# Four adds a batch between neighbouring u buffers: from GpSimd instructions to accumulating DMAs

## The chip, the cores and the metric

One core of one Trainium2 chip runs the whole program. The metric is the device time of one execution, in microseconds (us). The profile gives a span (first to last instruction) of one profiled execution and that execution's own time beside it.

## What is computed

One decoder layer over x of 16 batches x 224 tokens x 512 features, in fp32, with a layer norm after each of three sublayers:

- a selective state-space block: in-projection to 1024 channels (xi) and 1024 gates (z), a causal convolution of four taps, silu, then per channel d and state n (16 states) the scan `h[t] = exp(delta[t] * A[d, n]) * h[t-1] + delta[t] * B[t, n] * xc[t, d]` and the output `y[t, d] = sum over n of h[t] * C[t, n]`, plus `xc * Dp`, times silu(z), then the out-projection;
- a context sublayer: a projection of the rows plus a decayed running sum over the context rows;
- a mixture of 8 experts with top-1 routing: each token's row is scattered to its expert's slots, two matrix products with a relu between them, the results scattered back.

The change lies in `y[t, d] = sum over n`. The sum over the 16 states is taken as 4 groups of 4 states, and each group's products `h * C` are summed by TensorE into a PSUM bank with an identity matrix as weights.

## The kernel before

The program works through the batches in steps. In one step, the scan of batch b, the projections of batch b+1, the output side of batch b-1 and the routing of batch b-2 run beside each other; `run_steps` unrolls the steps, and each engine's `body(b, par)` weaves its share of the scan (`main`, once for each of 32 slots) with side jobs. The order on each engine is fixed by hand: tables `PE_AT`, `ACT_AT`, `DVE_AT` and `POOL_AT` give each side job the slot after which it is issued (`woven`, `together`). Once the batches are done, the experts follow (from about 1,920 us on), and the change touches nothing there.

A slot s is one of KB = 8 channel blocks (k = s // 4) times Q = 4 groups of four states (q = s % 4). All its tiles are 128 partitions x 896 fp32 (four states x 224 tokens), 448 KB, 3,584 bytes in each partition. For every slot:

- POOL (GpSimd) writes `u = dx * B` into one of UB = 6 buffers (L968). The buffer is that of slot s - 6; the wait ahead of it is `sum_done >= b*32 + s - 5`, so the sums through slot s - 6 must be done (the count moves by one for each slot).
- ACT writes the four decays into the PSUM ring (L817).
- DVE runs the scan (L1260) and then the product with C back into the u buffer (L1269). For the seven slots in `POOLED` (1, 5, 9, 13, 17, 21, 25) DVE leaves the states in the u buffer, and POOL makes the product two slots later, after it has made u(s+2) (L973).
- PE sums the slot into its y bank with matmuls of the identity (L1585, eight records for each slot); the last of them moves `sum_done`.

For the four slots in `ADDED` (5, 9, 13, 17) POOL adds the neighbour's product: right behind its own product of slot a it adds u(a-1) onto u(a) (L979), once its own product is written (`multiplied`) and DVE's product of slot a-1 is there (`product_made(pool, b, s - 3)`). PE then leaves slot a-1 out (L1581 returns from `main`), sums slot a alone and moves `sum_done` by 2. So u(a+5), which goes into the buffer of slot a-1, waits for PE's sum of slot a.

`product_made(eng, b, s)` is the wait for a slot's product: `pooled_ready` for the seven slots, `p_ready` for the others. PE calls it for every slot that it sums; ACT only for slots outside POOLED (for those inside it waits for the scan); SP for slots 28 to 31. POOL's queue also issues two indirect DMAs a batch, the scatter of the routed rows (L930), and in the experts the scatter of results (L992). SP's queue issues all loads: among them `in_x` (448 KB) once a batch around slot 12 and eight of `bc_rows` (448 KB each) around the end of a batch. Around the scan POOL also makes delta in four pieces (L897, L899, L901, L904; three of them at slots 4, 4 and 12, in `late_steps`), the context rows (L942) and the normalised rows (L952).

Of the kernel before, what the change touches and what calls it, by code (L numbers as in the profile page):

```python
# [14 lines left out]
def build_decoder(nc, t):  # L15
# [5 lines left out]
    ALU, ACT, AX = mybir.AluOpType, mybir.ActivationFunctionType, mybir.AxisListType.X  # L21
# [25 lines left out]
    u_of = lambda b, s: (b * SLOTS + s) % UB  # L47
# [10 lines left out]
    with ctx:  # L58
# [79 lines left out]
        def flat(name):  # L138
            o, n = plan[name]
            return arena[:, o:o + n]  # L140

        bc = flat("bc").rearrange("p (w n l) -> p w n l", w=2, n=NS)
        u = flat("u").rearrange("p (k n l) -> p k n l", k=UB, n=QN)
        u_flat = flat("u").rearrange("p (k m) -> p k m", k=UB)
# [33 lines left out]
        for g in range(NG):  # L178
# [54 lines left out]
        bc_loaded = [sem(f"bc_loaded{q}") for q in range(Q)]  # L233
        sp_step, sp_ready, dl_step, delta_done = map(sem, (
            "softplus_step", "softplus_ready", "delta_step", "delta_done"))
        decay_ready, u_ready, scan_done, p_ready, pooled_ready, sum_done, y_done, skip_ready, multiplied, y_plain = map(sem, (
            "decay_ready", "u_ready", "scan_done", "p_ready", "pooled_ready", "sum_done", "y_done", "skip_ready", "pooled_multiplied",
            "y_written_whole"))
        x_res_loaded, ctx_loaded, ctx_step, ctx_ready = map(sem, ("x_res_loaded", "ctx_loaded", "ctx_step", "ctx_ready"))
        g_exp = sem("depool_exp")  # L240
# [13 lines left out]
        def need(eng, s, value):  # L254

            if not isinstance(value, int) or value > 0:
                eng.wait_ge(s, value)

        def apart(eng):


            eng.sem_inc(wait_kept, 1)
# [71 lines left out]
        def job_copied(eng, step, name):  # L334

            k, before_it = job(step, name)
            eng.wait_ge(w_free[k], before_it + 1)
# [13 lines left out]
        def stages(step):  # L351

            if isinstance(step, int):
                return 0 <= step + 2 < NB, 0 <= step + 1 < NB, 0 <= step < NB, 0 <= step - 1 < NB, 0 <= step - 2 < NB
            return True, True, True, True, True

        POOLED = tuple(range(1, SLOTS - Q, 4))
        MADE = SLOTS - len(POOLED)
        ADDED = (5, 9, 13, 17)
        made = lambda s: s + 1 - sum(p <= s for p in POOLED)  # L360
        pooled = lambda s: sum(p <= s for p in POOLED)

        def product_made(eng, b, s):

            if s in POOLED:
                eng.wait_ge(pooled_ready, b * len(POOLED) + pooled(s))
            else:
                need(eng, p_ready, b * MADE + made(s))

# [520 lines left out]
        @block.gpsimd  # L890
        def _(pool):
            def make_delta(tt, j, par):

                n, k = tt * 12 + 3 * j, slice(2 * j, 2 * j + 2)
                relu, corr = (delta[:, k], dx[:, k]) if j < PAIRS - 1 else (sp3[:, 0], sp3[:, 1])
                pool.wait_ge(sp_ready, tt * 2 + (j // 2 + 1))
                nc.gpsimd.tensor_tensor(w1p[:, k], w1p[:, k], corr, ALU.subtract).then_inc(dl_step, 1)  # L897
                pool.wait_ge(dl_step, n + 1)
                nc.gpsimd.tensor_tensor(delta[:, k], relu, w1p[:, k], ALU.add).then_inc(dl_step, 1)  # L899
                pool.wait_ge(dl_step, n + 2)  # L900
                nc.gpsimd.tensor_tensor(dx[:, k], delta[:, k], xc[:, par, k], ALU.mult).then_inc(dl_step, 1)  # L901
                pool.wait_ge(dl_step, n + 3)
                apart(pool)
                nc.gpsimd.memset(delta[:, k, 0:1], BIG_STEP).then_inc(delta_done, 1)  # L904

            def side(b, par):
                pre, pro, scan, epi, tail = stages(b)
                nxt, e, e2 = b + 1, b - 1, b - 2

                def late_steps():  # L910

                    for j in (1, 2, 3):
                        yield f"delta{j}"
                        make_delta(b, j, par)

                def first_steps():

                    yield "delta0"
                    make_delta(nxt, 0, 1 - par)

                def scatter():

                    yield "scatter"
                    pool.wait_ge(rt_step, e2 * 13 + 13)
                    job_copied(pool, b, "rank")
                    pool.wait_ge(normed, e2 * 2 + 2)
                    pool.wait_ge(token_set, e2 + 1)
                    apart(pool)
                    for h in range(2):
                        nc.gpsimd.indirect_dma_start(  # L930
                            out=xe_dram, out_offset=bass.IndirectOffsetOnAxis(ap=slot_i[:, h:h + 1], axis=0),
                            in_=x2e[:, h, :], in_offset=None, bounds_check=E * CAP - 1, oob_is_err=False,
                        ).then_inc(scattered, 16)

                def context():

                    yield "ctx"
                    pool.wait_ge(ctx_step, e * 11 + 8)
                    if isinstance(b, int) and b == 1:
                        pool.wait_ge(s_wrest, 16 * 6)  # L940
                    v = ctxt[0:H, :, 0:D]
                    nc.gpsimd.tensor_tensor(v, v, g_bc[:].unsqueeze(1).to_broadcast([H, 2, D]), ALU.mult).then_inc(ctx_ready, 1)  # L942

                def next_rows():

                    yield "xn"
                    pool.wait_ge(rinv_ready, b + 3)
                    if pro:
                        k, n = job(b, "z3")
                        pool.wait_ge(w_full[k], n + 1)  # L950
                        apart(pool)
                    nc.gpsimd.tensor_tensor(xn, xT, rinv[:, 1:2, :].to_broadcast([P, DC, L]), ALU.mult).then_inc(xn_ready, 1)  # L952

                return together(POOL_DRAIN if not scan and not pre else POOL_AT, *(part() for part, there in (
                    (late_steps, scan), (first_steps, pro), (scatter, tail), (context, epi), (next_rows, pre)) if there))

            def body(b, par):
                def main(s):

                    k, q = s // Q, s % Q  # L960
                    need(pool, sum_done, b * SLOTS + s - UB + 1)
                    if isinstance(b, int) and b == 0 and s == 0:
                        pool.wait_ge(s_rows, 16)
                    if s < Q:
                        pool.wait_ge(bc_loaded[q], b * 32 + 32)
                    if s % (2 * Q) == 0:
                        pool.wait_ge(delta_done, b * 4 + (s // (2 * Q) + 1))
                    nc.gpsimd.tensor_tensor(u[:, u_of(b, s)], dx[:, k:k + 1, :].to_broadcast([P, QN, L]),  # L968
                                            bc[:, 0, q * QN:(q + 1) * QN, :], ALU.mult).then_inc(u_ready, 1)
                    if s - 2 in POOLED:  # L970
                        q = (s - 2) % Q
                        pool.wait_ge(scan_done, b * SLOTS + (s - 1))
                        nc.gpsimd.tensor_tensor(u[:, u_of(b, s - 2)], u[:, u_of(b, s - 2)], bc[:, 1, q * QN:(q + 1) * QN, :], ALU.mult  # L973
                                                ).then_inc(pooled_ready if s - 2 not in ADDED else multiplied, 1)
                    if s - 2 in ADDED:
                        pool.wait_ge(multiplied, b * len(ADDED) + (ADDED.index(s - 2) + 1))
                        apart(pool)
                        product_made(pool, b, s - 3)
                        nc.gpsimd.tensor_tensor(u[:, u_of(b, s - 2)], u[:, u_of(b, s - 2)], u[:, u_of(b, s - 3)], ALU.add  # L979
                                                ).then_inc(pooled_ready, 1)  # L980

                woven(side(b, par), main, stages(b)[2])

            run_steps(pool, body)

            pool.wait_ge(out0_stored, NB * 32)
            def expert(e, par):
                pool.wait_ge(ids_ready, e + 1)
                for m in range(CM):
                    pool.wait_ge(mm_step, e * (3 * CM) + (3 * m + 3))  # L990
                    apart(pool)
                    nc.gpsimd.indirect_dma_start(  # L992
                        out=out_rows, out_offset=bass.IndirectOffsetOnAxis(ap=ids[:, par, m:m + 1], axis=0),
                        in_=res[m], in_offset=None, bounds_check=NB * L - 1, oob_is_err=False,
                    ).then_inc(out_scattered[m % 2], 16)

            with pool.Fori(0, E - 1, 2) as i:
                expert(i, 0)
                expert(i + 1, 1)
# [742 lines left out]
```

## Time and profile before

| | us |
|---|---|
| runs | 2616.44, 2612.46, 2616.50 (median 2616.44) |
| the profiled execution | 2609.2 |
| its span | 2607.4 |
| busy over the span: PE / DVE / POOL / ACT | 2414.4 / 2080.3 / 1786.6 / 1751.3 |
| mean granted TensorE clock | 0.963 |

Busy shares over the whole span mix two stages: the batches (to about 1,900 us), in which PE, DVE and POOL all work, and the experts behind them, in which PE alone is full. They are to be read stage by stage. A wait row reads: engine and line that waited, after the arrow the one that ended the wait, then the total us, how often, and the longest.

### The profile page before, as it was taken

What the parts mean: (1) busy time and instruction counts of PE and PEld (TensorE: products, weight loads), DVE (VectorE), ACT (ScalarE), POOL (GpSimd) and SP (SyncE); (2) the same over time, 40 slices, a digit from 0 to 9 for tenths busy, and PEclk for the clock granted to TensorE, in tenths of its full rate; (3) what the DMA queues carried; (4) which work ended last, traced back from release to release, by engine and by line L of the source; (5) the groups of instructions that cost most, each with busy time, mean ns of one, the idle gap of its engine ahead of it and who ended that gap; (6) DMA issues with size and microseconds to landing.
All of it is one profiled execution on the core that took longest, in us unless ns stands there. A gap on an engine that the chain in (4) does not pass through costs nothing.

```text
span 2607.4 us, 33255 instructions
## 1 busy us (share of the span) xinstructions
PE 2414.4 (93%) x11291; PEld 2048.7 (79%) x11291; DVE 2080.3 (80%) x2288; ACT 1751.3 (67%) x4011; POOL 1786.6 (69%) x1044
## 2 busy tenths in 40 slices
PE   6788999999999999999999999997869999999997
PEld 6686887878778787877878787775659999999996
DVE  4998999999999999999999999998633455444452
ACT  5667888888888888888888888886533333333331
POOL 1989999999999999999999999999410101000100
PEclk9898999999999999999999999997979999999998
DMA  6041202203021220202113020220233333234320
GB/s 212 8 144 56 85 16 85 81 27 93 15 85 43 65 89 12 92 16 85 59 49 89 12 93 18 75 82 19 96 108 124 130 126 126 97 129 138 136 75 18
DMA packets 90852, 202.62 MB, mean 78 GB/s; under 512 B 7948, under 2 KB 16794, under 8 KB 90702
## 3 DMA queue, kind: packets, MB, share of 16 engines
q1 hardware_dynamic: 81486, 179.21, 21.3%
q0 software_dynamic: 5120, 14.21, 1.7%
q10 hardware_dynamic: 4096, 7.34, 0.9%
q8 instruction: 77, 1.26, 0.2%
q14 instruction: 73, 0.60, 0.1%
HBM read 171.32 MB, written 29.95 MB: 77 GB/s over the span
## 4 chain that ended last, share of the span: by engine, by line
POOL 40%; PE 37%; DVE 8%; issue 6%; ACT 5%; DMA 3%; SPq 0%; POOLq 0%; DVEq 0%; ACTq 0%
POOL arena L968 23%; PE work L1604 12%; PE ring L1604 11%; POOL arena L973 6%; PE y L1585 4%; POOL arena L979 4%; DVE ring L1260 4%; PE work L1393 3%; DMA arena<-bc_rows 3%; POOL arena L901 2%; POOL arena L899 2%; POOL arena L897 2%; PE work L1416 2%; ACT ring L817 2%; DVE arena L1269 2%
## 5 line engine op out<-in xcount | busy, mean ns | idle before, releaser
L968 POOL TENSOR_TENSOR arena<-arena 128x896 f32<-128x896 f32 x512 | 1056.6, 2090 | 15.8 <-DMA arena<-bc_rows 10.5
L817 ACT ACTIVATE ring<-arena,small 128x224 f32<-128x224 f32 x2048 | 794.9, 436 | 146.0 <-DVE arena L1269 114.9
L1585 PE MATMUL y<-arena,cst_sb 128*128 128x224 f32 x3584 | 772.2, 367 | 91.7 <-POOL arena L979 64.9
L1260 DVE TENSOR_TENSOR_SCAN ring<-ring,arena 128x896 f32<-128x896 f32 x400 | 809.3, 2023 | 50.3 <-POOL arena L968 32.5
L1585 PEld LDWEIGHTS y<-arena,cst_sb 128*128 128x128 f32 x3584 | 694.2, 197 | 162.8 <-POOL arena L979 73.5
L992 POOL DMA_INDIRECT out<-res,ids x32 | 46.8, 1463 | 638.1 <-DVE mst L1317 539.2
L1269 DVE TENSOR_TENSOR arena<-ring,arena 128x896 f32<-128x896 f32 x400 | 433.5, 1084 | 6.0
L1393 PE MATMUL work<-arena 128*128 128x224 f32 x2000 | 417.3, 365 | 6.7 <-DVE arena L1058 5.6
L1393 PEld LDWEIGHTS work<-arena 128*128 128x128 f32 x2000 | 390.9, 198 | 18.8 <-POOL arena L952 6.2
L1332 DVE SCALAR_TENSOR_TENSOR hidden_lo<-work,hidden_hi 128x448 fp32r<-128x448 f32 x128 | 80.0, 625 | 343.4 <-ACT hidden_hi L867 343.4
L867 ACT ACTIVATE hidden_hi<-work 128x448 fp32r<-128x448 f32 x128 | 69.8, 545 | 367.7 <-PE work L1604 367.7
L1260 DVE TENSOR_TENSOR_SCAN arena<-ring,arena 128x896 f32<-128x896 f32 x112 | 225.6, 2014 | 14.4 <-POOL arena L968 8.8
L973 POOL TENSOR_TENSOR arena<-arena 128x896 f32<-128x896 f32 x112 | 233.9, 2088 | 4.3 <-DVE arena L1260 4.2
L1416 PE MATMUL work<-arena 128*112 128x512 f32 x496 | 220.5, 592 | 0.0
L1604 PE MATMUL ring<-hidden_hi,weights_hi 128*128 128x448 f32 x512 | 189.4, 370 | 0.0
L1604 PE MATMUL work<-xe_hi,weights_hi 128*128 128x448 f32 x512 | 187.8, 367 | 1.3 <-DVE xe_lo L1295 1.3
L1604 PE MATMUL work<-xe_lo,weights_hi 128*128 128x448 f32 x512 | 187.5, 366 | 0.0
L1604 PE MATMUL work<-xe_hi,weights_lo 128*128 128x448 f32 x512 | 187.4, 366 | 0.0
L1604 PE MATMUL ring<-hidden_hi,weights_lo 128*128 128x448 f32 x512 | 187.0, 365 | 0.0
L1604 PE MATMUL ring<-hidden_lo,weights_hi 128*128 128x448 f32 x512 | 186.9, 365 | 0.0
L1416 PEld LDWEIGHTS work<-arena 128*112 128x112 f32 x496 | 87.9, 177 | 102.5 <-issue 101.9
L1282 DVE TENSOR_TENSOR weights_lo<-weights,weights_hi 128x2048 fp32r<-128x2048 f32 x64 | 146.0, 2284 | 1.2 <-ACT weights_hi L831 1.2
(208 smaller groups left out, 3297.7 us busy)
## 6 DMA issues: line engine op xcount, KB each, us to landing
weights<-in_w SPq DMA_DIRECT2D x64, 1024.0 KB, 7.2
arena<-bc_rows SPq DMA_DIRECT2D x128, 448.0 KB, 4.4
arena<-in_ctx SPq DMA_DIRECT2D x16, 896.0 KB, 5.7
expert_rows<-x2e SPq DMA_DIRECT2D x1, 7224.0 KB, 29.9
xrow<-expert_rows SPq DMA_DIRECT2D x8, 903.0 KB, 11.5
arena<-in_xT SPq DMA_DIRECT2D x16, 448.0 KB, 6.3
arena<-in_x SPq DMA_DIRECT2D x16, 448.0 KB, 3.6
out<-arena ACTq DMA_DIRECT2D x32, 224.0 KB, 2.3
```

The costliest lines, as they stand in the source:

```text
L817: last = nc.scalar.activation(decays[s % 2][:, i * L:(i + 1) * L], delta[:, k, :], ACT.Exp, scale=a_neg[:, n:n + 1])
L968: nc.gpsimd.tensor_tensor(u[:, u_of(b, s)], dx[:, k:k + 1, :].to_broadcast([P, QN, L]), bc[:, 0, q * QN:(q + 1) * QN, :], ALU.mult).then_i ...
L973: nc.gpsimd.tensor_tensor(u[:, u_of(b, s - 2)], u[:, u_of(b, s - 2)], bc[:, 1, q * QN:(q + 1) * QN, :], ALU.mult).then_inc(pooled_ready if ...
L979: nc.gpsimd.tensor_tensor(u[:, u_of(b, s - 2)], u[:, u_of(b, s - 2)], u[:, u_of(b, s - 3)], ALU.add).then_inc(pooled_ready, 1)
L1260: nc.vector.tensor_tensor_scan(states, h, u_flat[:, u_of(b, s), :], 0.0, ALU.mult, ALU.add).then_inc(scan_done, 1)
L1269: nc.vector.tensor_tensor(u[:, u_of(b, s)], h.rearrange("p (n l) -> p n l", n=QN), bc[:, 1, q * QN:(q + 1) * QN, :], ALU.mult).then_inc(p_ ...
L1282: nc.vector.tensor_tensor(r32(lo), w, hi, ALU.subtract).then_inc(ready, 1)
L1332: nc.vector.scalar_tensor_tensor(r32(h_lo[:, f % HR, :]), h_bank[f % 2][:, 0:CAP], 0.0, h_hi[:, f % HR, :], ALU.max, ALU.subtract).then_in ...
L1393: last = nc.tensor.matmul(bank[:, i * L:(i + 1) * L], w_in[:, c, o:o + P], xn[:, c, :], start=(c == 0), stop=(c == DC - 1))
L1416: last = nc.tensor.matmul(bank[0:H, 0:D], gate[:, 1 - par, k, h * H:(h + 1) * H], w_out[:, k, :], start=(k == 0), stop=(k == KB - 1))
L1585: last = nc.tensor.matmul(o, ident, u[:, u_of(b, s), i, :], start=False, stop=(q == Q - 1 and i == QN - 1), skip_group_check=True)
L1604: last = nc.tensor.matmul(out, r32(a), r32(b), start=(first and k == 0), stop=(stop and k == n - 1))
```

## The change

POOL no longer runs the add. After the same waits it issues an accumulating DMA from buffer u(a-1) onto u(a), whose landing moves a new semaphore `added` by 16; whoever needs slot a's product waits for that one. `pooled_ready` now counts the three slots (1, 21, 25) whose product isn't added to. Before a DMA is issued POOL waits until the one before it has landed.

```diff
-        decay_ready, ..., skip_ready, multiplied, y_plain = map(sem, (
+        decay_ready, ..., skip_ready, multiplied, added, y_plain = map(sem, (
...
         ADDED = (5, 9, 13, 17)
         made = lambda s: s + 1 - sum(p <= s for p in POOLED)
-        pooled = lambda s: sum(p <= s for p in POOLED)
+        ALONE = tuple(s for s in POOLED if s not in ADDED)
 
         def product_made(eng, b, s):
 
-            if s in POOLED:
-                eng.wait_ge(pooled_ready, b * len(POOLED) + pooled(s))
+            if s in ADDED:
+                eng.wait_ge(added, (b * len(ADDED) + (ADDED.index(s) + 1)) * 16)
+            elif s in POOLED:
+                eng.wait_ge(pooled_ready, b * len(ALONE) + sum(p <= s for p in ALONE))
             else:
                 need(eng, p_ready, b * MADE + made(s))
...
                         pool.wait_ge(multiplied, b * len(ADDED) + (ADDED.index(s - 2) + 1))
                         apart(pool)
                         product_made(pool, b, s - 3)
-                        nc.gpsimd.tensor_tensor(u[:, u_of(b, s - 2)], u[:, u_of(b, s - 2)], u[:, u_of(b, s - 3)], ALU.add
-                                                ).then_inc(pooled_ready, 1)
+                        need(pool, added, (b * len(ADDED) + ADDED.index(s - 2)) * 16)
+                        pool.dma_start(u_flat[:, u_of(b, s - 2), :], u_flat[:, u_of(b, s - 3), :], accum_op=ALU.add).then_inc(added, 16)
```

## Rows read from the trace of the kernel before

**Rows 1.** Busy time of each engine in the steady stretch of the batches.

```profile
core 0: us, PE busy (x) PEld busy (x) DVE busy (x) ACT busy (x) POOL busy (x), PEclk, DMA share, GB/s
200.00:1750.00 1550.00, 1481.77 (x6708) 1217.44 (x6708) 1498.31 (x1604) 1300.50 (x3176) 1492.46 (x864) 0.98 0.19 57
```

**Rows 2.** Waits of PE and of DVE in the same stretch.

```profile
PE y L1585 <- POOL arena L979: 32.8, 20, 7.6
DVE ring L1260 <- ACT ring L817: 16.2, 30, 3.2
DVE ring L1260 <- POOL arena L968: 14.7, 23, 1.7
```

**Rows 3.** Waits of POOL for the sums, over the whole span.

```profile
POOL arena L968 <- PE y L1585: 4.9, 4, 1.6
```

**Rows 4.** Where the adds of line L979 lie (min/median/max ns, first and last start).

```profile
L979 POOL TENSOR_TENSOR arena<-arena x64: 2071/2085/2101, 90.4 to 1819.5; 128x896 f32<-128x896 f32 x64
```

**Rows 5.** POOL in order of time, slots 7 to 22 of one batch (start, us, instructions).

```profile
763.15 2.08 POOL L973 TENSOR_TENSOR arena<-arena 128x896 f32<-128x896 f32 x1
765.41 2.08 POOL L979 TENSOR_TENSOR arena<-arena 128x896 f32<-128x896 f32 x1 [0.18 <-POOL arena L973]
767.44 8.22 POOL L968 TENSOR_TENSOR arena<-arena 128x896 f32<-128x896 f32 x4
777.89 2.09 POOL L979 TENSOR_TENSOR arena<-arena 128x896 f32<-128x896 f32 x1 [0.18 <-POOL arena L973]
779.94 2.09 POOL L968 TENSOR_TENSOR arena<-arena 128x896 f32<-128x896 f32 x1
785.76 6.20 POOL L968 TENSOR_TENSOR arena<-arena 128x896 f32<-128x896 f32 x3
806.67 2.09 POOL L979 TENSOR_TENSOR arena<-arena 128x896 f32<-128x896 f32 x1 [0.18 <-POOL arena L973]
```

**Rows 6.** PE in order of time in the same batch.

```profile
762.65 3.27 PE L1393 MATMUL work<-arena 128*128 128x224 f32 x16
767.54 3.29 PE L1585 MATMUL y<-arena,cst_sb 128*128 128x224 f32 x16 [1.61 <-POOL arena L979]
782.49 1.68 PE L1585 MATMUL y<-arena,cst_sb 128*128 128x224 f32 x8
784.00 3.60 PE L1416 MATMUL work<-arena 128*112 128x512 f32 x8
796.31 3.29 PE L1585 MATMUL y<-arena,cst_sb 128*128 128x224 f32 x16 [1.18 <-POOL arena L979]
```

**Rows 7.** PE in two stretches of the second half of that batch.

```profile
809.00:830.00 21.00, 21.00 (x113) 20.33 (x112) 20.90 (x18) 19.18 (x52) 20.55 (x12) 1.00 0.08 23
830.00:870.00 40.00, 39.71 (x177) 32.39 (x176) 38.76 (x43) 32.48 (x79) 38.37 (x26) 1.00 0.43 133
```

**Rows 8.** DMA issues of 448 KB: engine, count, KB each, median us from issue to landing.

```profile
arena<-bc_rows SPq DMA_DIRECT2D x128, 448.0 KB, 4.4
arena<-in_x SPq DMA_DIRECT2D x16, 448.0 KB, 3.6
```

**Rows 9.** The issue of one `in_x` load, and the DMA share in the slices behind it.

```profile
906.41 0.33 SPq L450 DMA_DIRECT2D arena<-in_x  x1
...
907.00:908.00 1.00, 1.00 (x8) 0.72 (x7) 0.79 (x1) 1.00 (x4) 1.00 (x2) 1.00 0.57 58
908.00:909.00 1.00, 1.00 (x8) 1.00 (x7) 1.00 (x1) 1.00 (x4) 1.00 (x1) 1.00 0.97 365
909.00:910.00 1.00, 1.00 (x7) 1.00 (x6) 1.00 (x4) 1.00 (x4) 1.00 (x2) 1.00 0.12 39
```

**Rows 10.** The indirect DMAs on POOL (min/median/max ns).

```profile
L930 POOL DMA_INDIRECT expert_rows<-x2e,slot_i x32: 941/958/4335, 372.6 to 1917.9; - x32
```

**Rows 11.** The last scatter of the program, and the DMA share until the span ends.

```profile
2602.84 0.94 POOL L992 DMA_INDIRECT out<-res,ids  x1 [2.77 <-issue]
...
2604.00:2605.00 1.00, 0.00 (x0) 0.00 (x0) 0.00 (x0) 0.00 (x0) 0.00 (x0) 0.50 0.63 186
2605.00:2606.00 1.00, 0.00 (x0) 0.00 (x0) 0.00 (x0) 0.00 (x0) 0.00 (x0) 0.50 0.12 43
```

More of the change, by code:

```diff
@@ L235, in build_decoder @@
             "softplus_step", "softplus_ready", "delta_step", "delta_done"))
-        decay_ready, u_ready, scan_done, p_ready, pooled_ready, sum_done, y_done, skip_ready, multiplied, y_plain = map(sem, (
-            "decay_ready", "u_ready", "scan_done", "p_ready", "pooled_ready", "sum_done", "y_done", "skip_ready", "pooled_multiplied",
+        decay_ready, u_ready, scan_done, p_ready, pooled_ready, sum_done, y_done, skip_ready, multiplied, added, y_plain = map(sem, (
+            "decay_ready", "u_ready", "scan_done", "p_ready", "pooled_ready", "sum_done", "y_done", "skip_ready", "pooled_multiplied", "pairs_added",
             "y_written_whole"))
```

## The prediction

> **What bounds the kernel now.** I read the busy time by stage first. In the steady stretch of the batches PE is busy 1481.8 of 1550 us, DVE 1498.3 and POOL 1492.5 [rows 1]: 95.6%, 96.7% and 96.3%. Three engines are full together, so work taken from POOL alone can give back at most what the other two idle. One batch takes 112.5 us: the first add starts at 90.4 and the last at 1819.5, the last one lies 41.3 us behind the first of its own batch (806.67 - 765.41), and 15 batches lie between: (1729.1 - 41.3) / 15 [rows 4, 5]. DVE's idle share of 3.3% is 3.7 us of it, PE's of 4.4% is 5.0 us.
>
> Next the waits. DVE waited 14.7 us for u and 16.2 us for the decays in 13.8 batches; PE waited 32.8 us for the adds, in 20 of the some 55 that lie in the stretch [rows 2]; POOL waited for a sum in only 4 of 512 slots [rows 3]. The six u buffers were thus enough, but by little: in the order shown next the sum is done 2.4 us before POOL asks for it.
>
> Last the order in time around an add. At slot 7 POOL's product ends at 765.2, the add runs from 765.41, u(8) starts at 767.44 and u(10) two instructions later, at 771.55 (each of the four takes 2.06) [rows 5]. So 6.15 us lie between the start of the add and the start of u(10), the first that needs the sum of slot 5. PE ran that sum at 767.54, having stood idle for 1.61 us, and took 1.65 for it (16 records in 3.29, two slots) [rows 6].
>
> **The change part by part.**
>
> *Removed:* four adds a batch of 2.09 us, 8.3 us of POOL's 112.5 [rows 4].
>
> *Added on POOL:* four issues. No row shows a direct or accumulating DMA issued by POOL. The nearest is the indirect DMA, 0.96 us [rows 10], over 112 rows of about 2 KB where this one has 128 of 3.5 KB. I take 0.96; above, the same instruction was once stretched to 4.33 us, while DVE was in the weight splits of the experts; below, an issue on SP takes 0.33 [rows 9]. The 0.18 us wait for the product's write stays. The wait for the add before costs nothing: that landed at least 6 us earlier, since the adds are 12.5 us apart (765.41 and 777.89) [rows 5]. POOL gains 1.1 us at each add, 4.5 a batch, if nothing stands in its way.
>
> *Added, the landing time L*, from the start of the issue until `added` moves. It is the number that decides, and no row shows it. Lower end: the accumulate goes like a plain copy. `in_x`, the same 448 KB, lands 3.6 us after its issue on SP [rows 8]; with POOL's issue of 0.96 in place of 0.33 that is 4.2. Upper end: twice the slower plain load of the same shape, 2 x 4.4 [rows 8], plus 0.6, is 9.4. Between them, from parts: `in_x` kept the 16 engines busy for 0.57 + 0.97 + 0.12 = 1.7 us [rows 9]. An accumulate must read two tensors and write one, so I double this: 3.3. The fixed part: the last scatter of the program starts its issue at 2602.84, and the span ends at 2607.4, which is 4.56 us, of which 0.75 are engine time (0.63 + 0.12) [rows 11], leaving 3.8; but part of this is the program's end. From `in_x` the fixed part is 3.6 - 1.7 + 0.6 = 2.5. L is then between 5.8 and 7.1; I take 6.3, nearer to the load, which ran in the midst of the batches as the adds will.
>
> *What POOL pays for L.* The start of the add to the start of u(a+5) takes 6.15 us now. Afterwards it takes L + 1.65 (PE's sum, when PE stands waiting), or 0.96 + 4.11 = 5.07 if that is longer. The difference is L - 4.5: at L = 4.5 nothing is gained or lost, and at 6.3 each such add costs 1.8 us. That holds at slots 5, 13 and 17. Behind slot 9's add the three delta instructions of `late_steps` (779.94 + 2.09 to 785.76, 3.7 us) lie between u(12) and u(13) [rows 5] and cover the landing, so that add gives its 1.1 us back in full. Sum for a batch: 3 x 1.8 - 1.1 = 4.3 us.
>
> *What PE pays.* PE obeys its order: while it waits for `added`, the side jobs behind that sum stand (the out-projection after slots 6 and 7, dt and z after 14 and 15), and so do ACT's and DVE's parts of these jobs. At slot 5 PE was free at 765.9 (762.65 + 3.27) [rows 6]; it now waits until 771.7, against 767.54: 4.2 us late. At slot 9 it had no wait (it came at 782.49, when the add was over since 779.98) [rows 5, 6]; it comes 4.2 later and again finds the sum ready. At 13 it comes before the landing again. In the rest of the batch it can't catch up: 21.0 of 21 us and 39.7 of 40 are busy [rows 7]. PE's idle time at the adds is about 9 to 10 us a batch by this count, and its busy time 107.5 (95.6% of 112.5): together 117, the same as POOL's 112.5 + 4.3. Two engines give the same period, so I let no other idle time absorb it.
>
> *Elsewhere.* The DMA engines have room: their share is 0.19 [rows 1]. The four transfers move the equivalent of 4 x 3.3 = 13 us a batch of 16-engine time, 12%. `in_x` is issued around the third of them and may hold it up by its own 1.7 us in some batches; not counted. ACT and SP wait for no added slot. The wait of `sum_done` at the y banks (gates) follows PE's shift and is in it. The experts are untouched: nothing.
>
> **Sum.** 16 batches x 4.3 = 69 us on top of the profiled execution's 2609: 2678. That execution was 7 us faster than the median of the runs (2616), so 2678 is 2.4% above the median, and the forecast holds with either base.
>
> By the Trainium skill's page "DMA: Bandwidth & Descriptors", section on the anatomy of one DMA on the GpSimd path, a DMA takes 2.0 us plus its bytes over 436 GB/s; for 458,752 bytes that is an estimate of 3.05 us. With such an L, even with an issue of 0.96 ahead of it, every add would gain 1.1 us or nearly so, and the sum would be a gain of some 40 us. The rows don't support it whole: the plain `in_x` load already took 3.6 [rows 8], and the page's formula says nothing of an accumulate.
>
> **The rivals.**
>
> *A. Forecast: L from 5 to 8.* For it: the parts above. 3 x (L - 4.5) - 1.1 gives from 0.4 to 9.4 us a batch, 2615 to 2760. Chance 0.58.
>
> *B. The accumulate is as quick as a copy (L below 4.7): faster.* Place: the stretch from the add's start to u(a+5) on POOL; it decides below L = 4.8, where 3 x (L - 4.5) equals the 1.1 of slot 9. At 4.2 a batch gains 0.9 + 1.1 = 2.0 us, 32 in all: 2577. More than DVE's idle 3.7 us a batch, 59 us, can't come: 2550. For it: the engines moved 365 GB/s in the best slice of `in_x` [rows 9], and both tensors lie in SBUF. Against: a second read, and PE still waits longer than for POOL's add of 2.3 us. Chance 0.18. The skill's formula quoted above speaks for this one, and is in that chance.
>
> *C. The accumulate is slow (L over 8).* The add within the DMA engine may run far below its copy rate, or its issue on POOL is stretched as in the 4.33 us case [rows 10]. At 9.4 slot 9's cover is used up too (6.15 + 3.7 - 1.65 = 8.2), and a batch pays 3 x 4.9 + 1.2 = 15.9 us: 254 us, 2863. Chance 0.18.
>
> *D. Nothing to see (L about 4.8, or a loss that idle time takes up).* Three engines idle 3 to 4% each, and a stall that falls where POOL had run ahead of DVE costs nothing. 2609 to 2616. Chance 0.06.
>
> **How the numbers follow.** A measurement of this kernel can tell some 0.2%, 5 us, from no change. Faster by more than that: B, 0.18. Within it: D, 0.06. Slower: A and C, 0.76. The range takes all of A and D, the upper part of B (to 2590) and C up to 2860, its worked end: that leaves out about 0.1 on each side.
>
> **What the profile of the changed kernel would show.** Line L979 as 64 DMA issues of 448 KB on POOL's queue, with a landing time: 6.3 by my sum. The row on POOL for the issue: about 1 us. In the steady stretch, waits "PE y L1585 <- DMA" near 130 us (9 to 10 us a batch) where 32.8 us were put down to POOL's add [rows 2]; waits "POOL L968 <- PE y L1585" at slots 10, 18 and 22, which had all but none, near 5 us a batch. POOL's busy share in the steady stretch falls from 96% to about 89%, DVE's from 97% to about 93%. The adds' distance from batch to batch goes from 112.5 to 117. What would make me wrong: a landing under 4.5 us, or POOL still never waiting for sums (then the buffers had more slack than the one batch shows), or an issue of several us, which would put the cost on POOL itself.

## The result, and the profile after

The changed kernel takes 2689.8 us (median of 4 runs, 2688.9 to 2691.4) against 2616.0 before: 1.029 times, 95% interval 1.027 to 1.030, 74 us slower. The forecast was 2678 with a range of 2590 to 2860. Sign and size hold. The reason given for the size does not: the landing time, from the start of a DMA's issue until its semaphore moves, was taken too long, and what makes up for it was not in the sum.

Busy time in the steady stretch, to be read beside [rows 1]:

```profile
core 0: us, PE busy (x) PEld busy (x) DVE busy (x) ACT busy (x) POOL busy (x), PEclk, DMA share, GB/s
200.00:1750.00 1550.00, 1447.48 (x6427) 1191.14 (x6426) 1441.39 (x1551) 1246.35 (x3051) 1374.65 (x831) 0.95 0.27 73
```

POOL fell from 96.3% to 88.7% and DVE from 96.7% to 93.0%, as forecast. No engine is busy for more than 93.4% now, and the period of a batch is longer. PE's granted clock is 0.95 of full where it was 0.98.

The waits in that stretch, of PE, POOL, DVE and ACT in this order; the first answers to the first of [rows 2], the second to [rows 3]:

```profile
PE y L1587 <- DMA arena<-arena: 81.2, 39, 9.7
POOL arena L970 <- PE y L1587: 80.3, 41, 3.9
POOL arena L982 <- POOL arena L975: 22.0, 33, 0.9
DVE ring L1262 <- ACT ring L819: 52.7, 48, 3.2
DVE arena L1122 <- PE work L1418: 19.6, 11, 3.4
ACT dbl L741 <- PE work L1482: 70.4, 13, 5.6
```

Before, POOL's wait for the sums was 3.9 us in this stretch, DVE's for the decays 16.2, and ACT's for PE's side job xp 39.2:

```profile
ACT dbl L739 <- PE work L1480: 39.2, 14, 5.6
```

The add itself, and its transfer from issue to landing; [rows 4 and 8] show the instruction that it replaces and the plain loads:

```profile
L982 POOL DMA_DIRECT2D arena<-arena x64: 877/884/1113, 91.5 to 1897.4; - x64
DMA to landing us min/median/max: 4.2/4.3/5.4
```

The landing is 4.3 us in the median, at the lower end of the prediction's bounds (4.2 to 9.4). One batch in order of time, POOL first, then PE, to be laid beside [rows 5, 6]:

```profile
793.04 2.07 POOL L975 TENSOR_TENSOR arena<-arena 128x896 f32<-128x896 f32 x1
795.79 0.99 POOL L982 DMA_DIRECT2D arena<-arena  x1 [0.68 <-POOL arena L975]
796.44 4.47 POOL L970 TENSOR_TENSOR arena<-arena 128x896 f32<-128x896 f32 x2
803.60 4.13 POOL L970 TENSOR_TENSOR arena<-arena 128x896 f32<-128x896 f32 x2 [2.68 <-PE y L1587]
...
842.40 0.89 POOL L982 DMA_DIRECT2D arena<-arena  x1 [0.94 <-POOL arena L975]
```

```profile
800.16 4.86 PE L1587 MATMUL y<-arena,cst_sb 128*128 128x224 f32 x16 [3.03 <-DMA arena<-arena]
...
831.87 6.06 PE L1587 MATMUL y<-arena,cst_sb 128*128 128x224 f32 x16 [2.54 <-DMA arena<-arena]
```

The DMA is issued at 795.79 and PE's sum starts at 800.16. But u(10) starts only at 803.60, 7.81 us after the issue; the prediction had 6.3 + 1.65 = 7.95. The 16 records of two sums, 3.29 us before, take 4.86 and 6.06. The granted clock in the slices tells why (PE busy, clock, DMA share, GB/s):

```profile
795.00:796.00 1.00, 1.00 (x4) 0.50 0.00 0
796.00:797.00 1.00, 1.00 (x5) 0.72 0.00 0
797.00:798.00 1.00, 0.13 (x1) 1.00 0.81 154
798.00:799.00 1.00, 0.00 (x0) 1.00 1.01 190
799.00:800.00 1.00, 0.00 (x0) 0.98 0.64 115
800.00:801.00 1.00, 0.84 (x2) 0.50 0.00 0
801.00:802.00 1.00, 1.00 (x4) 0.50 0.00 0
802.00:803.00 1.00, 1.00 (x5) 0.50 0.00 0
803.00:804.00 1.00, 1.00 (x6) 0.81 0.00 0
```

The clock was at its lower level (1.2 GHz) during PE's work ahead of the wait, rose, and after PE had stood idle for 3 us fell again for 3.4 us, of which PE worked 3.2. The sum of slot 5 took 3.35 us, about twice its time. How long PE had waited does not say by itself whether the clock falls. Of the 39 waits for the landing in the steady stretch 19 were followed by a sum at the lower level, wholly or in part: 9 of 14 at slot 5, 9 of 13 at slot 13, 1 of 12 at slot 17. A wait of 3.20 us (ended at 1153.16) was followed by full speed, one of 1.30 us (ended at 362.92), with full speed ahead of it, by half. In the kernel before it was 5 of 20 waits for the add.

The transfer held the 16 engines for 0.81 + 1.01 + 0.64 = 2.5 us, where the prediction had 3.3.

By the starts of the adds, a batch takes (1805.9 - 46.6) / 15 = 117.3 us now (1897.4 - 91.5, less 842.40 - 795.79), against 112.5: 4.8 us a batch, 77 in 16 batches, are the whole loss. The distances from add to add, each the mean of twelve batches (the third to the fourteenth) by POOL's order in time:

| | 5 to 9 | 9 to 13 | 13 to 17 | 17 to the next 5 | sum |
|---|---|---|---|---|---|
| before | 12.50 | 16.29 | 12.54 | 71.19 | 112.5 |
| after | 14.00 | 15.76 | 15.01 | 72.47 | 117.2 |
| difference | +1.50 | -0.53 | +2.47 | +1.28 | +4.7 |
| prediction | +1.8 | -1.1 | +1.8 | +1.8 | +4.3 |

### The profile page after: what moved, and what is told of

It reads as the page before. It is cut to its first block, busy times and chain, and to the rows that moved or that the text cites. A ratio compares the mean times of both kernels' runs of the same rounds, so it can differ in the third digit from the quotient of the medians.

```text
span 2687.1 us, 33318 instructions
## 1 busy us (share of the span) xinstructions
PE 2447.8 (91%) x11291; PEld 2076.4 (77%) x11291; DVE 2084.4 (78%) x2288; ACT 1750.5 (65%) x4011; POOL 1715.1 (64%) x1044
## 4 chain that ended last, share of the span: by engine, by line
PE 52%; POOL 19%; DMA 9%; DVE 9%; ACT 5%; issue 5%; SPq 0%; POOLq 0%; DVEq 0%; ACTq 0%
PE y L1587 14%; PE work L1606 12%; PE ring L1606 11%; POOL arena L970 10%; DMA arena<-arena 6%; PE work L1395 6%; POOL arena L975 4%; PE work L1418 4%; DVE ring L1262 3%; DMA arena<-bc_rows 2%; DVE arena L1271 2%; ACT ring L819 2%; POOL arena L903 1%; POOL arena L901 1%; POOL arena L899 1%
## 5 line engine op out<-in xcount | busy, mean ns | idle before, releaser
L970 POOL TENSOR_TENSOR arena<-arena 128x896 f32<-128x896 f32 x512 | 1079.3, 2164 | 113.3 <-PE y L1587 100.4
L1587 PE MATMUL y<-arena,cst_sb 128*128 128x224 f32 x3584 | 795.7, 376 | 152.0 <-DMA arena<-arena 129.9
L1587 PEld LDWEIGHTS y<-arena,cst_sb 128*128 128x128 f32 x3584 | 714.1, 203 | 229.9 <-DMA arena<-arena 144.5
L1395 PE MATMUL work<-arena 128*128 128x224 f32 x2000 | 426.5, 371 | 6.0 <-DVE arena L1060 5.7
L1395 PEld LDWEIGHTS work<-arena 128*128 128x128 f32 x2000 | 399.6, 202 | 17.2 <-issue 6.3
L975 POOL TENSOR_TENSOR arena<-arena 128x896 f32<-128x896 f32 x112 | 234.1, 2090 | 10.7 <-DVE arena L1262 10.7
```

The source lines that it names most:

```text
L1395: last = nc.tensor.matmul(bank[:, i * L:(i + 1) * L], w_in[:, c, o:o + P], xn[:, c, :], start=(c == 0), stop=(c == DC - 1))
L1587: last = nc.tensor.matmul(o, ident, u[:, u_of(b, s), i, :], start=False, stop=(q == Q - 1 and i == QN - 1), skip_group_check=True)
```

## The experiments

Two theories stood at first. *Landing:* the loss is the landing time, as POOL pays it through the buffers. *PE:* the loss is that PE stands in its order, with the clock that it loses and the side jobs that it holds up. The texts put ahead of the runs number theories of their own. Times on different chips are compared by their loss against the kernel before on the same chip; for the changed kernel that is 74 us.

### PE kept busy while it waits

```diff
+                    for _ in range({5: 12, 13: 12, 17: 3}.get(s, 0)):
+                        nc.tensor.matmul(yb[(k // 2) % 2][:, 2 * L:2 * L + 64], ident, ident[:, 0:64], start=False, stop=False,
+                                         skip_group_check=True)
                     product_made(pe, b, s)
```

> The changed kernel with matmuls of no use ahead of PE's wait at the added slots: 12 of 64 columns at slots 5 and 13, 3 at slot 17, about 2.4 us each time, shorter than the 3.0 and 2.5 us that PE stood idle there. Theory 1 (idle PE loses its clock: the sums behind the wait took 4.86 and 6.06 us where they took 3.29, at a granted clock of 0.5): the clock stays up, a sum of one slot goes back from about 3.2 us to 1.65, POOL starts u(10) and u(18) some 1.5 us earlier, 3 us a batch, about 2640 us. Theory 2 (the landing alone costs, the clock is a by-product): no change or a little slower, 2690 to 2700.

2695.5 us, 1.032 (1.030 to 1.034), a loss of 83 us: no gain. The clock mostly came back: 0.97 over the steady stretch, 8 of 22 waits still followed by a sum at the lower level, and in the batch shown the sums at full speed and POOL's wait at u(10) down to 1.10 us from 2.68.

```profile
802.17 2.79 PE L1586 MATMUL y<-cst_sb 128*128 128x64 f32 x24
805.50 3.29 PE L1590 MATMUL y<-arena,cst_sb 128*128 128x224 f32 x16 [0.54 <-DMA arena<-arena]
...
POOL arena L970 <- PE y L1590: 86.5, 42, 4.6
ACT dbl L741 <- PE work L1482: 70.1, 13, 5.6
```

But over all batches POOL's wait for sums stayed (86.5 us), and ACT waited as long as before for xp (70.1): a filler keeps PE's speed, not its place in the order. Theory 1 as I put it, with some 50 us to be had by the clock alone, falls. The fillers also cost PE time wherever it would not have waited, so this run doesn't price the clock by itself, and no other does. By an estimate from the rows above, 19 sums lengthened by up to 1.6 us each are at most 30 us in the steady stretch of the changed kernel, 2.2 us a batch, if nothing hid them. The clock thus stays open as a part of the loss.

### Seven u buffers

```diff
-    UB = 6
+    UB = 7
```

> The changed kernel with seven u buffers instead of six, so that u(a+5) goes into the buffer of slot a-2, whose sum PE has done before it waits for the DMA. POOL no longer waits for the late sum. Theory 1 (the cost reaches the end through POOL's wait for the buffer, 80.3 us in the steady stretch, where it was 3.9): nearly the whole loss of 74 us comes back, 2610 to 2625. Rival (PE's own order is the bound: it still stands for the landing and loses its clock): at most a third comes back, 2665 or more, and PE's waits for the DMA stay near 80 us.

2681.5 us, 1.026 (1.023 to 1.028): 8 us below the changed kernel, but a loss of 69 us on its own chip, so 4 to 8 us of 74 come back, and the intervals of the two kernels still touch. The rival holds on the time; PE's waits for the DMA fell to 63.9 us, where it had said near 80. The control with the kernel before:

> Control: the kernel before with seven u buffers. POOL waited only 4.9 us in total for sums, so nothing should move: 2608 to 2618. If it gains as much as the changed kernel did (8 to 14 us), then the buffers had nothing to do with the DMAs.

2614.8 against 2615.4, 1.000 (0.999 to 1.001): there the seventh buffer changes nothing. In the changed kernel it took POOL's wait for the sums to 9.3 us, and another took its place:

```profile
POOL arena L970 <- PE y L1587: 9.3, 19, 1.0
POOL arena L975 <- DVE arena L1262: 75.0, 35, 4.4
DVE ring L1262 <- ACT ring L819: 56.4, 44, 3.2
ACT dbl L741 <- PE work L1482: 71.4, 13, 5.6
```

Read upwards, as one chain that these rows suggest and do not prove: PE is late with xp, since it stood at slot 5; ACT waits for xp in its order (up to 5.6 us) and is late with the next decays; DVE waits for these; POOL waits for DVE's scan before its product, issues the add late, and PE stands again at slot 13.

### xp issued earlier on PE

```diff
-    UB = 6
+    UB = 7
...
-"out1.2": 9, "out1.3": 9.01, "xp": 10,
+"out1.2": 9, "out1.3": 9.01, "xp": 8.9,
```

> The changed kernel with seven u buffers, and with PE's side job xp issued ahead of the last two pieces of the out-projection (due 8.9 instead of 10) so that it is 3.4 us earlier. Theory (with seven buffers the late landing reaches the end through PE's late xp: ACT stands 5.6 us for it in order, the next decays are late, DVE's scan waits 3.1 us for them and POOL 3.9 us for the scan): ACT's wait for xp falls from 71 us to under 30, and the time from 2681 to about 2640. Rival (PE's lost clock or another side job sets the period): 2670 or more.

2676.9 us, 1.025 (1.023 to 1.027), within reach of the 2681.5 of seven buffers alone. ACT's wait for xp is gone from the list, as forecast, and the time did not follow. Other side jobs of PE take its place: DVE waits for the ranks (L1164) and the out-projection (L1122), and ACT for dt (L1406), 54.1 us where it was 14.9 with seven buffers alone. And slot 13, where PE had all but no wait with seven buffers (0.4 us), is a place of waiting again (28.9), at half clock each time.

```profile
DVE work L1164 <- PE work L1473: 38.9, 12, 4.8
DVE arena L1122 <- PE work L1418: 37.2, 23, 3.8
PE y L1587 <- DMA arena<-arena: 79.4, 27, 10.7
```

> Control: the kernel before with xp at 8.9 on PE. ACT waited 39 us for xp in the steady stretch; if this wait is on the path there too, 2590 to 2605; if another wait takes its place (three engines are busy 96 to 97%), 2608 to 2618.

In the kernel before, the same move gave 2614.8 against 2615.4, 1.000 (0.999 to 1.001): nothing on the path there either.

### PE sums the next slot first

```diff
-                    if s + 1 in ADDED:
+                    if s + 1 in ADDED or s in ADDED:
                         return
-                    product_made(pe, b, s)
+                    for slot in (s, s - 1) if s - 1 in ADDED else (s,):
+                        product_made(pe, b, slot)
...
-                    last.then_inc(sum_done, 2 if s in ADDED else 1)
+                    last.then_inc(sum_done, 3 if s - 1 in ADDED else 1)
```

> The changed kernel, but PE sums slot a+1 ahead of slot a at the four added slots, and moves sum_done by 3 behind both. No wait is taken away; PE has 1.65 us of useful work while the DMA runs. Theory 1 (PE's idle time and the clock that goes with it are the cost): PE's waits for the DMA fall from 81 us in the steady stretch to about 25, the sums run at full clock, 2640 us. Theory 2 (the landing time alone sets when u(a+5) can start): the landing stays 4.3 us and u(a+5) starts as late as now: 2675 to 2690.

2707.7 us, 1.035 (1.032 to 1.038): slower than both theories had it. PE's waits for the DMA fell to 66.0 us only, where 25 were forecast. At slot 9, where PE had never stood for the landing, its sum now comes behind 28 records of the out-projection, and POOL, with six buffers, waits for it:

```profile
809.25 12.18 PE L1418 MATMUL work<-arena 128*112 128x512 f32 x28
821.27 3.19 PE L1588 MATMUL y<-arena,cst_sb 128*128 128x224 f32 x16
...
824.54 4.13 POOL L970 TENSOR_TENSOR arena<-arena 128x896 f32<-128x896 f32 x2 [2.56 <-PE y L1588]
```

### PE goes on with its side jobs

Only slots 5 and 13 are put off, that of slot 5 behind the first piece of the out-projection.

```diff
-                    if s + 1 in ADDED:
+                    if s + 1 in ADDED or s in (5, 13):
                         return
+                    for slot, done in {6: ((6, 0),), 7: ((5, 3), (7, 1)), 14: ((14, 0), (13, 3))}.get(s, ((s, 2 if s in ADDED else 1),)):
```

> The changed kernel, PE's order changed at two slots: the sum of slot 5 stands behind slot 6's sum and the first piece of the out-projection, that of slot 13 behind slot 14's. The two next sums of slots 9 and 17 stay. PE has 3.4 and 1.65 us of its own work under the two landings. Theory (the loss is PE's standing idle in its order and what stands behind it): PE's waits for the DMA fall from 81 to about 30 us in the steady stretch, the granted clock rises, the period falls by 3 to 4 us: 2625 to 2645. Rival (the landing itself and six buffers set the pace through POOL): 2675 or more, with POOL's waits for the sums at 80 us or above.

> As pe_goes_on, with seven u buffers, so that neither POOL's wait for the late sum nor PE's idle time is left at slots 5 and 13. Theory: both costs gone, 2605 to 2625, level with the kernel before; if below 2605, the freed 4 x 2.09 us of POOL shows for the first time. Rival (some other chain): 2650 or more.

With six buffers 2701.3 us, 1.034 (1.032 to 1.035), the worst but one, and the rival's case; with seven 2638.9, 1.012 (1.009 to 1.015; one of its four runs took 2656.5), which neither the theory (2605 to 2625) nor the rival (2650 or more) had. Waits of PE and POOL, first with six, then with seven buffers:

```profile
PE y L1588 <- DMA arena<-arena: 84.0, 40, 3.8
POOL arena L970 <- PE y L1588: 94.1, 40, 4.6
```

```profile
PE y L1588 <- DMA arena<-arena: 57.3, 27, 4.3
POOL arena L970 <- PE y L1588: 31.1, 21, 3.4
```

This is the result that settles most. Losses against the kernel before on the same chip: 74 us for the changed kernel, 69 with the seventh buffer alone, 89 with the new order alone, and 26 with both. So each alone brings next to nothing or costs, and both together give 47. A late landing has at least two ways to the end: through the buffers to POOL, and through PE's order to ACT and DVE.

The new order did not shut the second way; it moved the place. PE's waits for the landing by slot in the steady stretch, in us, and the median landing at slot 13 (it is 4.3 at the other slots in all four):

| | 5 | 9 | 13 | 17 | sum | landing at 13 |
|---|---|---|---|---|---|---|
| changed kernel | 45.2 | 0 | 18.0 | 18.0 | 81.2 | 4.7 |
| seven buffers | 51.0 | 0 | 0.4 | 12.5 | 63.9 | 4.3 |
| new order, six | 0.9 | 14.9 | 35.4 | 32.8 | 84.0 | 5.5 |
| new order, seven | 1.6 | 0.3 | 44.3 | 11.1 | 57.3 | 6.2 |

Of the 57.3 us that are left, 44.3 are at slot 13. There the transfer meets the load `in_x`, the one term that the prediction named and didn't count. From one batch with the new order and seven buffers:

```profile
805.22 0.53 SPq L452 DMA_DIRECT2D arena<-in_x  x1
805.92 0.90 POOL L982 DMA_DIRECT2D arena<-arena  x1 [1.08 <-issue]
811.20 1.78 PE L1588 MATMUL y<-arena,cst_sb 128*128 128x224 f32 x8 [2.74 <-DMA arena<-arena]
```

With seven buffers alone `in_x` is issued 2.6 to 3.6 us after the add in 14 of 16 batches, and the add lands in 4.2 to 4.6; here the two are issued within 0.7 us of each other in the same 14 batches, and it lands in 5.2 to 7.4. No run moved `in_x` by itself, so what share of the 26 us it has is not shown.

### Which of the four adds costs

The kernel before, with only some of the adds made by DMA (`BY_DMA` in place of `ADDED` in the wait and in the issue):

```diff
+        BY_DMA = (9,)          # or (5,), or (9, 13, 17)
...
+                        if s - 2 in BY_DMA:
+                            need(pool, added, (b * len(BY_DMA) + BY_DMA.index(s - 2)) * 16)
+                            pool.dma_start(..., accum_op=ALU.add).then_inc(added, 16)
+                        else:
                             nc.gpsimd.tensor_tensor(..., ALU.add).then_inc(pooled_ready, 1)
```

> Of the four adds only that of slot 9 is a DMA; those of 5, 13 and 17 are POOL instructions again. Slot 9 is the one whose landing lies under the three delta instructions and at whose sum PE never stood. Theory (a DMA costs only where PE reaches the sum before it lands): nothing lost; POOL's start-to-start distance from slot 9 to 13 falls by 0.5 us as in the changed kernel, so 2605 to 2615. Rival (each accumulating DMA costs a quarter of the loss, wherever it is): 2630 or more.

> Of the four adds only that of slot 5 is a DMA. Its sum is one at which PE stands for the landing (3.0 us in the batch shown, 1.6 before). Theory (the cost lies only where PE reaches the sum before the landing, and is about the same at each such place): the 74 us come from slots 5, 13 and 17, so about a third of it here, 2635 to 2645. Rival (PE has enough idle time in a batch, 5 us, to absorb one such stall; only several together cost): 2612 to 2622.

> Slots 9, 13 and 17 are added by DMA, slot 5 by POOL: the complement of dma_at_five, which cost 62 of the 74 us. Theory (slot 5 is the costly place, for behind it PE's order holds the out-projection and xp, for which DVE and ACT stand in theirs; behind 13 and 17 it holds less): the rest of the loss, 12 us, so 2612 to 2630. Rival (the stalls overlap: any one place at which PE stands brings nearly the whole loss, and the others then add nothing): 2655 to 2680.

| adds by DMA | us | against before, same chip | ratio (95%) |
|---|---|---|---|
| 9 | 2612.4 | 2615.4 | 0.999 (0.998 to 1.000) |
| 5 | 2674.8 | 2612.5 | 1.023 (1.021 to 1.025) |
| 9, 13, 17 | 2675.6 | 2613.8 | 1.023 (1.021 to 1.025) |
| 5, 9, 13, 17 | 2689.8 | 2616.0 | 1.029 (1.027 to 1.030) |

Slot 9 costs nothing, as forecast, though its DMA lands in the same 4.3 us: PE waited for it 1.6 us in the whole stretch. That much of the theory is right. The price is not shared out over the others as I had it: slot 5 alone makes 62 us, the three others together 62, all four 74. My expectations of 2635 to 2645 and of 2612 to 2630 both missed; the rival of the last, that the stalls overlap, holds. PE's waits, with slot 5 alone and with the three others:

```profile
PE y L1592 <- DMA arena<-arena: 52.2, 14, 9.5
```

```profile
PE y L1592 <- DMA arena<-arena: 70.0, 30, 4.7
...
820.40 4.42 POOL L971 TENSOR_TENSOR arena<-arena 128x896 f32<-128x896 f32 x2
828.80 4.12 POOL L971 TENSOR_TENSOR arena<-arena 128x896 f32<-128x896 f32 x2 [3.98 <-PE y L1592]
```

With slot 5 by DMA, PE had no wait at slots 9, 13 and 17 in any batch of the stretch: it was late there already. Without it, PE comes to slot 13 early and stands there, 53.9 us in 13 batches where the changed kernel has 18.0. One lateness covers the next. Two things besides the order differ in this run, though: its add of slot 13 is issued within half a microsecond of `in_x` in most batches and lands in 5.4 us (median) instead of 4.7, and the sum behind it ran at the lower clock 13 times out of 13. Its 62 us are thus not the price that these three adds have in the changed kernel.

### What the accumulate costs

```diff
-..., u_flat[:, u_of(b, s - 3), :], accum_op=ALU.add).then_inc(added, 16)
+..., u_flat[:, u_of(b, s - 3), :]).then_inc(added, 16)
```

> The changed kernel with a plain copy on the same queue in place of the accumulate; the products of slots 5, 9, 13 and 17 are left out of the output, since their neighbours' are written over them. It prices the accumulate itself. If the second read costs as much again as the copy, the engine time of one transfer falls from 2.46 us to about 1.3 and the landing from 4.3 to about 3.1 us; the time then falls by 3 x 1.2 us a batch, to about 2630. If the accumulate is nearly free, the landing stays above 4.0 and the time at 2690.

This kernel leaves out the products of four slots. One run: 2633.9 us, 22 above the median of before on that chip, and 56 below the changed kernel (52 by the losses).

```profile
L982 POOL DMA_DIRECT2D arena<-arena x64: 577/579/747, 91.6 to 1842.5; - x64
DMA to landing us min/median/max: 2.7/2.8/5.4
```

The engines' time for one copy (PE busy, clock, DMA share, GB/s), and the totals of POOL's queue (packets, MB, share of 16 engines) with the copies and with the accumulates (1.7% in the kernel before, which has neither):

```profile
548.00:549.00 1.00, 1.00 (x6) 1.00 0.57 229
549.00:550.00 1.00, 0.00 (x1) 1.00 0.58 229
q0 software_dynamic: 10240, 43.58, 4.6%
q0 software_dynamic: 14336, 43.57, 7.7%
```

The issue takes 0.58 us instead of 0.88 and the landing 2.8 instead of 4.3: adding costs 1.5 us a transfer. Of this, 1.3 are engine time: the copy holds the 16 engines for 0.57 + 0.58 = 1.15 us, the accumulate for 2.5. That is what the expectation gave for a second read that costs as much again (1.3 us, a landing of 3.1, about 2630). The time follows by 52 to 56 us for 64 transfers that land 1.5 us earlier. Only 4 of 19 waits for it were followed by a sum at the lower clock, so part of this can be the clock's. And a landing of 2.8 us, well below the 4.5 at which an add at slot 5, 13 or 17 breaks even in the prediction's formula (4.87 for the whole batch), is still slower than POOL's own add.

## Why the prediction was right or wrong

**Bound.** Three engines are full together, and there is thus little to gain from POOL: right. POOL lost 7.6 points of busy share and nothing was gained.

**Issue.** 0.96 us taken, 0.88 measured. But the term was more than the issue: POOL stands 0.68 us instead of 0.18 behind its product ahead of the DMA, and the u behind it is stretched (two take 4.47 instead of 4.12 us). From the product's end to u(9)'s end are 5.8 us (795.11 to 800.91), against 6.4 before (765.23 to 771.6): POOL gains 0.6 a piece, not 1.1. Slot 9, the only undisturbed one, shows it in the table: -0.53 where -1.1 stood.

**Landing.** This is the step that failed: 6.3 us taken, 4.3 measured. Both parts were too long: engine time 2.5 for 3.3, and the fixed part 1.8 for 3.0. The doubling itself was sound (1.15 for the copy, 2.5 for the accumulate); its base was not, for it took the 1.7 us of `in_x`, a load from outside SBUF, for a transfer within it. The fixed part was taken between the last scatter, whose row holds the end of the program, and `in_x`, whose 2.5 is already too long; the plain copy has 2.8 - 1.15 = 1.65.

**The sum behind the wait.** Failed the other way: PE's sum was taken at 1.65 us, its length at full clock. In the batch shown it ran at half clock, and 3.44 us lie between its start (800.16) and u(10) (803.60); the start came 4.37 us after the issue. 1.9 us too many and 1.8 too few: so 7.81 us came out where 7.95 stood, and the wait ahead of the issue, longer by 0.5, comes on top. The near agreement at this place is an accident, and the sum of the batch agrees for reasons that were not in it. Of the 14 batches 5 had that sum at full clock, and in four of them that were read (issues at 329.77, 444.90, 1148.79 and 1264.39) u(10) starts 6.1 to 6.2 us after the issue, as early as before the change. With L = 4.3 and all else as written the formula 3 x (L - 4.5) - 1.1 gives a gain of 1.7 us a batch, 27 in all; that is rival B, and it would have been my forecast with a better landing time.

**Rival B** (L below 4.7: faster) had its condition met and its result refuted, by the change itself and more sharply by the plain copy, at 2.8 us and 22 us slower. The Trainium skill's page "DMA: Bandwidth & Descriptors", section on the anatomy of one DMA, had given an estimate of 3.05 us for these bytes; the plain copy, at 2.8, comes within 0.3 us of it, and the accumulate, at 4.3, lies 1.3 above it. What misled was not its figure but the break-even point that I put it against.

**PE's part.** Right in kind: the side jobs behind the sum held up, 81.2 us of waits in the stretch (about 130 forecast, so too high by half again), POOL's waits for sums 80.3 (5 us a batch, 69, forecast), a period of 117.3 (117 forecast). Wrong was the sentence that two engines which give the same period confirm it: they are two ways of one delay, and the price of each add is not its own, as the last experiments show.

**`in_x`.** Left out of the sum, and seen: 13 to 17 is the stretch with the largest excess, +2.47 for +1.8, the add of slot 13 lands in 4.7 us (median, longest 5.4) where the other three take 4.3, and `in_x` lands in 4.9 us where it took 3.6 [rows 8]. Where another kernel let the two fall further apart or closer together, the landing at 13 went from 4.3 to 6.2; no run was made for it alone.

## What to carry to other kernels

Moving 2 us of work from an engine to a DMA replaces a short operation by a long latency; ask who stands in order behind its result, not how busy the engine was. A formula that adds up such stalls can hit the total and be wrong in every place: do one of the four alone, and its complement, before believing in a price for each. When a late result can reach the end by two ways, removing either shows little; remove both, and look at each place afterwards, for a wait can have moved instead of gone.

## What the runs showed of the hardware

An accumulating DMA of 448 KB from one place in SBUF onto another lands 4.3 us after the start of its issue on POOL's queue, the plain copy 2.8; the issues take 0.88 and 0.58 us of POOL, and the transfers hold the 16 engines for 2.5 and 1.15 us. With seven buffers and PE's new order, an accumulate issued within 0.7 us of a load of the same size landed in 5.2 to 7.4 us. After waits of 0.5 to 9.7 us PE's granted clock stood at its lower level in 19 of 39 cases in the changed kernel, for 3.4 us each time at 363 and at 800 us; with 64-column matmuls of no use ahead of the waits it was 8 of 22. And POOL stands 0.5 us longer behind its own product ahead of a DMA than ahead of an add (0.68 against 0.18).
